# Transformer block and graph attention in fp32: the handover from attention to feed-forward reordered

## The reference

```python
# condition c: [B, 128]; mod gives shift, scale and gate for both halves
x = x + g_msa * attention(modulate(layernorm(x), sh_msa, sc_msa), W_qkv, W_out, b_out)
x = x + g_mlp * (gelu(modulate(layernorm(x), sh_mlp, sc_mlp) @ W1 + b1) @ W2 + b2)
# then a graph attention over the first 20 nodes with the integer mask adj [B, T, T, 11]:
#   twice: softmax(q k / sqrt(8) where adj.sum(-1) > 0, + adj @ w_bias) applied to the features, @ Wout
x = x + relu(self_feat + graph_attention_0 + graph_attention_1)
```

## Time and profile before

| | |
|---|---|
| median of 3 runs | 643.64 us (642.64 to 646.8) |
| profiled execution | 646.53 us, its span 645.0 us |
| TensorE busy | 626.7 us, 97% of the span |
| VectorE / ScalarE / GpSimd busy | 507.7 / 480.8 / 290.1 us |
| granted clock of TensorE over the span | 0.99 |
| handover looked at here | about 404 to 431 us |

### The profile page before, as it was taken

How to read it: one execution, slowest core, us unless ns; L and a number is a source line. 1 busy time by engine, 2 the same in 40 slices (tenths; PEclk the granted TensorE clock), 3 DMA queues, 4 the chain that set the end, 5 groups by cost and what they waited for, 6 DMA issues and landing times.

```text
span 645.0 us, 17285 instructions
## 1 busy us (share of the span) xinstructions
PE 626.7 (97%) x5560; PEld 542.2 (84%) x5560; DVE 507.7 (79%) x1116; ACT 480.8 (75%) x1722; POOL 290.1 (45%) x354
## 2 busy tenths in 40 slices
PE   8999999999999999999999999889998999999996
PEld 7778888888888888888888888779897888888875
DVE  4887887878788778878787886977866888888874
ACT  4888877877978878788779788768776565656552
POOL 3353444443452534544434524546554444554451
PEclk9999999999999999999999999999999999999996
DMA  7212011010110110110111102013341122112100
GB/s 240 61 29 54 10 46 44 18 44 22 38 44 8 44 52 8 44 44 17 44 28 33 44 1 63 25 59 111 101 135 59 45 67 67 43 55 65 49 27 24
DMA packets 54530, 32.50 MB, mean 50 GB/s; under 512 B 15184, under 2 KB 52320, under 8 KB 54496
## 3 DMA queue, kind: packets, MB, share of 16 engines
q1 hardware_dynamic: 52864, 27.85, 15.7%
q0 software_dynamic: 1632, 4.21, 2.0%
HBM read 25.74 MB, written 6.31 MB: 50 GB/s over the span
## 4 chain that ended last, share of the span: by engine, by line
PE 88%; DVE 6%; SPq 2%; ACT 2%; issue 1%; DMA 0%; ACTq 0%; DVEq 0%
PE banks L601 10%; PE banks L627 9%; PE banks L612 8%; PE banks L1890 7%; PE banks L572 6%; PE banks L576 4%; PE banks L573 4%; PE banks L1306 4%; PE banks L1862 3%; PE banks L585 3%; PE banks L1876 3%; PE banks L1850 2%; PE banks L648 2%; PE banks L649 2%; PE banks L587 2%; PE banks L650 2%
## 5 line engine op out<-in xcount | busy, mean ns | idle before, releaser
L518 POOL TENSOR_TENSOR late_blocks<-late_blocks,p_rsum 128x512 f32<-128x512 f32 x128 | 130.5, 1040 | 209.3 <-DVE p_rsum L934 209.3
L813 ACT ACTIVATE late_blocks<-banks,neg_max 128x128 f32<-128x128 f32 x512 | 182.8, 392 | 2.4 <-DVE neg_max L927 2.4
L813 ACT ACTIVATION_READ_ACCUMULATOR late_blocks<-banks,neg_max 128x1 f32 x512 | 119.1, 233 | 0.0
L791 ACT ACTIVATE wide<-banks 128x512 f32<-128x512 f32 x127 | 78.4, 618 | 38.8 <-PE banks L576 34.1
L947 DVE CAST oT_hi<-banks 128x512 fp32r<-128x512 f32 x60 | 41.5, 691 | 63.9 <-PE banks L627 63.9
L572 PE MATMUL banks<-xT_hi,w_qkv_hi 128*128 128x256 f32 x256 | 82.3, 322 | 0.6 <-DVE xT_lo L922 0.6
L927 DVE TENSOR_REDUCE neg_max<-banks 128x8 f32<-128x1024 f32 x64 | 77.1, 1205 | 1.2
L601 PE MATMUL banks<-wide 64*128 64x128 f32 x1024 | 74.4, 285 | 0.0
L576 PE MATMUL banks<-xT_hi,w_qkv_lo 128*128 128x256 f32 x256 | 71.5, 279 | 0.1
L573 PE MATMUL banks<-xT_lo,w_qkv_hi 128*128 128x256 f32 x256 | 71.3, 278 | 0.0
L601 PEld LDWEIGHTS banks<-wide 64*128 64x128 f32 x1024 | 62.1, 187 | 10.7 <-issue 7.9
(11 more groups left out here) (170 smaller groups left out, 1558.5 us busy)
## 6 DMA issues: line engine op xcount, KB each, us to landing
early<-in_mask SPq DMA_DIRECT2D x16, 220.0 KB
early<-in_mask SPq DMA_DIRECT2D x80, 44.0 KB
x_in<-in_x SPq DMA_DIRECT2D x16, 128.0 KB, 2.1
x_res<-in_x SPq DMA_DIRECT2D x16, 128.0 KB, 2.2
x_scratch<-x SPq DMA_DIRECT2D x16, 128.0 KB, 1.9
f_x_in<-x_scratch SPq DMA_DIRECT2D x16, 128.0 KB, 2.4
f_x_res<-x_scratch POOLq DMA_DIRECT2D x16, 128.0 KB, 2.8
x_scratch<-f_x POOLq DMA_DIRECT2D x16, 128.0 KB, 2.2
```

The costliest lines, as they stand in the source:

```text
L518: pool.tensor_tensor(p[:, par, heads, :], p[:, par, heads, :], p_rsum[:, par, heads].unsqueeze(2).broadcast_to([128, 4, T]), ALU.mult).the ...
L791: act.activation(dst, proj_ps[k % 2], ACT.Copy).then_inc(proj_saved[k % 2], 1)
L813: act.activation(p[:, par, m, :], s_ps[par][:, e, j, :], ACT.Exp, bias=neg_max[:, par, 4 * e + j:4 * e + j + 1], accum_out=p_sum[:, par, m ...
```

## The change

- Attention's last body, TensorE: `last_probs_v(1)` comes before `turn_back(LAST)`.
- The high parts of units 0 and 1 are made by ScalarE (`save_last_oT(0)`, `(1)`) behind `cast` and in front of the load of gelu's table; VectorE makes only the low parts, both in front of the residual. ScalarE's modulation of pair 0 now stands in front of the high parts of units 2 and 3.
- The second group of unit 3 is normalised by VectorE (`normalise_last`) instead of GpSimd.
- The row maximum of unit 2 comes before the moments of pair 0. The moments of pair 1 move behind the copies of units 2 and 3. The moments of pair 2 move from the feed-forward's body 0 to behind `gate(PAIRS)`, and `sum_cells` behind these. GpSimd makes both inverse deviations (pairs 1 and 2) before `weigh`.
- TensorE: `turn(pair(1))` comes before the first layer of pair 0, `turn_back(PAIRS)` behind it. ScalarE: `modulate` of pair 1 first in body 0. VectorE: `split` of pair 1 and then `residual(PAIRS)` first in body 0.
- `f_xT_hi` and `f_xT_lo` get two buffers, and `split` waits for the products of the pair before the last.
- SyncE: pair 2 is loaded without the wait for the 15 stores (it waits for three, earlier).

```diff
@@ -509,11 +510,11 @@
             pool.tensor_tensor(rstd[:], rstd[:], ln_const[:, 1], ALU.pow).then_inc(ln_rstd_made, 1)
-        def normalise(i, unit):
+        def normalise(i, unit, groups=2):
             par = unit % 2
             pool.wait_ge(rsum_ready, i * 4 + (unit + 1))
-            for grp in range(2):
+            for grp in range(groups):
                 heads = slice(4 * grp, 4 * grp + 4)
                 pool.tensor_tensor(p[:, par, heads, :], p[:, par, heads, :],
@@ -545,13 +546,13 @@
             ffn.parts["rstd_first"](pool)
             normalise(LAST, 2)
-            normalise(LAST, 3)
+            normalise(LAST, 3, groups=1)
             ffn.parts["rstd_second"](pool)
             edges.parts["weigh"](pool, LAST)
         run_bodies(pool, body, last_body)
-    def tensor(pe):
+    def tensor(pe, turn_back_only=False):
         def turn_x(i):
@@ -705,7 +706,10 @@
         def turn_last(unit, grp):
-            pe.wait_ge(p_ready, LAST * 8 + (2 * unit + grp + 1))
+            if grp == 1 and unit == 3:
+                pe.wait_ge(last_p_ready, 1)
+            else:
+                pe.wait_ge(p_ready, LAST * 8 + (2 * unit + grp + 1))
             if grp == 0 and unit == 0:
                 pe.wait_ge(turn_saved[0], LAST * 8 + 1)
@@ -749,8 +753,8 @@
             ffn.parts["turn_first"](pe)
             last_probs_v(0)
+            last_probs_v(1)
             turn_back(LAST)
-            last_probs_v(1)
             turn_last(2, 0)
             turn_last(2, 1)
@@ -758,6 +762,9 @@
             last_probs_v(3)
+        if turn_back_only:
+            turn_back(PAIRS)
+            return
         setup.tensor(pe)
         turn_x(-1)
@@ -783,7 +790,6 @@
         run_bodies(pe, body, last_body)
         project_out(PAIRS)
-        turn_back(PAIRS)
     def scalar(act):
@@ -856,6 +862,12 @@
                 save_v(i, V1[0], 1, 0)
+        def save_last_oT(unit):
+            half, b = unit // 2, unit % 2
+            act.wait_ge(turn_full[0], LAST * 8 + WEIGHTED[unit])
+            act.activation(oT_hi[:, 4 * half:4 * half + 4, b, :],
+                           last_ps[unit % 2].rearrange("p (c t) -> p c t", c=4), ACT.Copy).then_inc(oT_high, 1)
+
         def last_body():
@@ -864,18 +876,16 @@
             exps(LAST, 3, 0, 8)
             edges.parts["cast"](act, LAST)
+            save_last_oT(0)
+            save_last_oT(1)
             ffn.parts["load_gelu"](act)
             save_turned(LAST, 2)
...
             act.activation(last_pT[1][:, 4:8, :].rearrange("p m t -> p (m t)"), t_ps[1],
                            ACT.Copy).then_inc(turn_saved[1], 1)
-            for unit in (2, 3):
-                half, b = unit // 2, unit % 2
-                act.wait_ge(turn_full[0], LAST * 8 + WEIGHTED[unit])
-                act.activation(oT_hi[:, 4 * half:4 * half + 4, b, :],
-                               last_ps[unit % 2].rearrange("p (c t) -> p c t", c=4),
-                               ACT.Copy).then_inc(oT_high, 1)
             ffn.parts["modulate_first"](act)
+            save_last_oT(2)
+            save_last_oT(3)
         setup.scalar(act)
...
@@ -1031,18 +1041,23 @@
             src = last_ps[unit % 2].rearrange("p (c t) -> p c t", c=4)
             hi = oT_hi[:, 4 * half:4 * half + 4, b, :]
-            if unit < 2:
-                dve.wait_ge(turn_full[0], LAST * 8 + WEIGHTED[unit])
-                dve.tensor_copy(hi, src).then_inc(oT_high, 1)
             dve.wait_ge(oT_high, LAST * 4 + (unit + 1))
             dve.tensor_tensor(oT_lo[:, 4 * half:4 * half + 4, b, :], src, hi.bitcast(F32),
                               ALU.subtract).then_inc(turn_saved[0], 1)
+        def normalise_last():
+
+            dve.wait_ge(rsum_ready, LAST * 4 + 4)
+            heads = slice(4, 8)
+            dve.tensor_tensor(p[:, 1, heads, :], p[:, 1, heads, :],
+                              p_rsum[:, 1, heads].unsqueeze(2).broadcast_to([128, 4, T]),
+                              ALU.mult).then_inc(last_p_ready, 1)
+
         def last_body():
             invert_sums(LAST, 1)
+            row_max(LAST, 2)
             ffn.parts["moments_first"](dve)
-            row_max(LAST, 2)
             save_last(0, 0)
             save_last(0, 1)
@@ -1051,19 +1066,24 @@
             ffn.parts["normalise_first"](dve)
             invert_sums(LAST, 3)
+            normalise_last()
             gate(LAST)
             save_last_oT(0)
+            save_last_oT(1)
             residual(LAST)
-            save_last_oT(1)
             save_last(2, 0)
             save_last(3, 0)
-            edges.parts["sum_cells"](dve, LAST)
+            ffn.parts["moments_second"](dve)
             save_last_oT(2)
             save_last_oT(3)
             ffn.parts["split_first"](dve)
             gate(PAIRS)
+            ffn.parts["moments_third"](dve)
+            edges.parts["sum_cells"](dve, LAST)
+
+        if residual_only:
             residual(PAIRS)
-
+            return
         for n in range(2):
...
@@ -1152,8 +1173,8 @@
     gate_cols = sb("f_gate_cols", [128, 2, 2, COLS])
     xT = sb("f_xT", [128, 2, T])
-    xT_hi = sb("f_xT_hi", [128, 2 * T], F32R)
-    xT_lo = sb("f_xT_lo", [128, 2 * T], F32R)
+    xT_hi = sb("f_xT_hi", [128, 2, 2 * T], F32R)
+    xT_lo = sb("f_xT_lo", [128, 2, 2 * T], F32R)
     hT = g.wide[:, 0:2 * MCH * 2 * T].rearrange("p (n c t) -> p n c t", n=2, c=MCH)
@@ -1215,12 +1236,12 @@
         if first:
-            sp.wait_ge(g.x1_stored, 2 * 16)
+            sp.wait_ge(g.x1_stored, 3 * 16)
             load_x(Step(0, 0))
             load_x(Step(0, 1))
             return
+        body(Step(-1, 0))
         sp.wait_ge(g.x1_stored, (PAIRS - 1) * 16)
-        body(Step(-1, 0))
         store_last_x1(sp)
         run_bodies(sp, body, start=-1)
@@ -1241,7 +1262,7 @@
         def body(s):
-            if more(s, 2) and not at(s, -1):
+            if more(s, 2) and not at(s, 0):
                 rstd_of(step_from(s, 2))
             if more(s, -2):
@@ -1253,6 +1274,7 @@
         if part == "second":
             rstd_of(Step(0, 1))
+            rstd_of(Step(1, 0))
             return
         if part == "first":
@@ -1292,9 +1314,9 @@
             for c in range(first, first + 2):
                 dst, cols = hid_ps[s.par][:, c, :], slice(c * 128, c * 128 + 128)
-                pe.matmul(dst, g.w1_hi[:, cols], xT_hi[:], start=True, stop=False)
-                pe.matmul(dst, g.w1_hi[:, cols], xT_lo[:], start=False, stop=False)
-                last = pe.matmul(dst, g.w1_lo[:, cols], xT_hi[:], start=False, stop=True)
+                pe.matmul(dst, g.w1_hi[:, cols], xT_hi[:, s.par], start=True, stop=False)
+                pe.matmul(dst, g.w1_hi[:, cols], xT_lo[:, s.par], start=False, stop=False)
+                last = pe.matmul(dst, g.w1_lo[:, cols], xT_hi[:, s.par], start=False, stop=True)
             last.then_inc(hid_full, 1)
@@ -1318,10 +1340,12 @@
             if more(s, 0):
                 hidden(s, 0)
-            if more(s, 1):
+            if more(s, 1) and not at(s, 0):
                 turn(step_from(s, 1))
             if more(s, 0):
                 hidden(s, 2)
+            if at(s, 0):
+                turn_back_last(pe)
             if more(s, -2):
                 turn_back(step_from(s, -2))
@@ -1331,6 +1355,7 @@
             return
+        turn(pair(1))
         run_bodies(pe, body, stop=PAIRS - 1)
@@ -1399,9 +1424,11 @@
         def body(s):
+            if at(s, 0):
+                modulate(step_from(s, 1))
             if more(s, 0):
                 gelu(s, 0)
-            if more(s, 1):
+            if more(s, 1) and not at(s, 0):
                 modulate(step_from(s, 1))
             if more(s, 0):
@@ -1462,10 +1489,11 @@
             dve.wait_ge(modulated, s.n + 1)
-            zero_wait(dve, hid_full, s.n * 2)
-            dve.tensor_copy(xT_hi[:], flat).then_inc(xT_split, 1)
+            zero_wait(dve, hid_full, s.n * 2 - 2)
+            dve.tensor_copy(xT_hi[:, s.par], flat).then_inc(xT_split, 1)
             dve.wait_ge(xT_split, s.n * 2 + 1)
-            dve.tensor_tensor(xT_lo[:], flat, xT_hi[:].bitcast(F32), ALU.subtract).then_inc(xT_split, 1)
+            dve.tensor_tensor(xT_lo[:, s.par], flat, xT_hi[:, s.par].bitcast(F32),
+                              ALU.subtract).then_inc(xT_split, 1)
         def residual(s):
@@ -1488,7 +1516,10 @@
         def body(s):
-            if more(s, 2) and not at(s, -1):
+            if at(s, 0):
+                split(step_from(s, 1))
+                residual_last(dve)
+            if more(s, 2) and not at(s, 0):
                 moments(step_from(s, 2))
             if more(s, 1) and not at(s, 0):
@@ -1515,12 +1546,17 @@
             normalise(Step(0, 0))
             copy_cols(mod_cols, Step(0, 0), mod_cols_ready)
+            return
+        if part == "second":
             moments(Step(0, 1))
             return
...
             normalise(Step(0, 1))
             copy_cols(mod_cols, Step(0, 1), mod_cols_ready)
+            return
```

(2 more changed lines are left out.)

22 lines of the change are left out of this document (13 added, 9 removed).

## The result

The changed kernel takes **650.25 us** (median of 15 runs, 647.49 to 651.98); the kernel before, in runs on the same chip beside it, takes 645.08 us (15 runs, 642.64 to 648.33). The ratio is 1.0077 with an interval of 1.0061 to 1.0092: about 5.0 us slower, where 2.6 was forecast, and beyond the upper end of the range. The forecast of 646.2 stood on a median of three runs, 643.64; the median of 15 is 1.44 higher.

A forecast was written before the change was run, and what follows sets the result against it. TensorE, busy 97% of the span, was taken to bound, with the third pair's first products deciding. Part 1 gave 0; the held low part and late load gave +2.6 on 643.64: 646.2 us, range 643.0 to 648.0.

The forecast's parts named there:

- The base: Median time of the kernel before, 643.64 us, to which the forecast shift of 2.6 us was added.
- What bounds: Attention to feed-forward handover: when the third pair's first products start on TensorE decides; at most 4.11 us to gain.
- Part 1, gain 0: Both weighings at once, high parts on ScalarE: projection ends at 422.57 as before; 0.6 us gain without contention.
- one of the two orders that were named: VectorE beside GpSimd: normalising product held, or gate columns' copy behind it; both put the gating about 1.0 us later.
- The walk: Step-by-step times from the gating at 413.65 to the projection's end at 422.57; the 1.28 us table load costs nothing.
- Part 2, the held low part: VectorE's low part of the second pair's split, held by GpSimd's weighing, ends 427.34; products start 427.4, 0.35 us later.
- Part 3, the late load: Fourth pair's load, issued behind the last residual, puts the third pair's first products at 433.05 instead of 430.43: +2.6 us.
- landed + 2.4: Fourth pair's load lands 2.4 us, the median, after its issue at 428.2, so at 430.6.
- the 0.7 us more: Allowance for GpSimd's two residual loads sharing queues with the fourth pair's load; landings range from 2.1 to 3.1.
- rival "worse": GpSimd's loads push the landing past 3.1 us and two GpSimd products delay the gating: +4 and more; chance 0.06.
- TensorE's own work doesn't bind: Handover: products from 427.4 plus 3.40 us of TensorE's steps give 430.8, ahead of the third pair's split at 433.05.

The follow-up runs named there:

- e4_norm: Changed kernel with both groups of the last unit normalised on GpSimd again, none on VectorE; 649.75 us, ratio 1.01.
- e1_cells: Changed kernel with the sum of cells, and with it GpSimd's weighing, back ahead of the last two low parts; 645.99 us, ratio 1.0007.
- f1_warm: e10_hold_res plus one more 128 KB load that nothing reads, issued on SyncE's queue ahead of the last store; 648.72 us, ratio 1.005.
- c1_after: The changed kernel once more, unedited, for a second profile; 650.87 us, ratio 1.0075.
- e5_awake: Changed kernel with 18 unread identity products on TensorE in the pause behind the last pair's turn back; 649.56 us, ratio 1.0063.
- e3_cells_load: Changed kernel with the sum of cells and GpSimd's weighing moved back, and the fourth pair's load ahead of the last store; 642.56 us, ratio 0.9961.
- e7_all: Changed kernel with sum of cells and weighing moved back, fourth pair's load ahead of the last store, GpSimd normalising both groups; 641.52 us, ratio 0.9951.
- e8_res_early: Changed kernel with GpSimd's two residual loads issued before the third pair's inverse deviation; 648.44 us, ratio 1.0061.
- e10_hold_res: Changed kernel with GpSimd's two residual loads issued early and the fifth pair's load held until the fourth pair's moments are made; 649.07 us, ratio 1.0055.
- e9_hold_fifth: Changed kernel with the fifth pair's load held in SyncE's queue until the fourth pair's moments are made; 650.01 us, ratio 1.009.

## Why the prediction was wrong in size and right in mechanism

**The base.** 650.25 is 4.05 above the forecast of 646.2. 1.44 of it is the base, the median of three runs; the other 2.6 are the shift. Without either the base's 1.44 or the 1.63 of the landing below, the time would still lie above the range's end of 648.0, and without both inside it.

**What bounds: right.** When the third pair's first products start decided it; the distance explains 4.0 to 4.25 of the 5.0 us.

**Part 1, gain 0: right.** The gate columns' copy was held for 1.00 us behind the normalising product, one of the two orders that were named. TensorE's last projection product comes 0.64 us earlier than before (421.65 against 422.29), but at 402 us, where the two kernels still do the same, this execution is already 0.63 us ahead, so nothing was won. Without the contention it would have been 0.82 us (e4_norm), where 0.6 was forecast. The walk had the table load in front of the copy cost nothing; ScalarE's copy waits for TensorE (0.70 us) and not for the load, as said.

**Part 2, the held low part: right, to the tenth.** Forecast to end 0.29 us after the weighing, it ended 0.27 after it, and e1_cells shows the cause: 0.42 us without the weighing. The Trainium skill (SBUF — State Buffer, section "SBUF: two separate sides") calls it an exclusive lock for the whole instruction, between a VectorE instruction with two SBUF inputs and a GpSimd instruction that reads SBUF. The 2.04 agrees with that, as far as the start goes: the held subtraction ended 0.27 us behind the weighing, less than its own 0.42.

**Part 3, the late load: right in every step but one.** From the end of the last projection product (forecast 422.57, measured 421.93) the sum stands like this:

| step | forecast, us | measured, us |
|---|---|---|
| to the residual's end | 427.75 - 422.57 = 5.18 | 427.01 - 421.93 = 5.08 |
| to the load's issue | 0.46 | 0.50 |
| **landing** | **2.4** | **4.02** |
| statistics to the third pair's products | 2.45 | 434.04 - 431.53 = 2.51 |
| sum | 10.48 | 12.11 |

The whole miss of this sum, 1.63 us, is **the term "landed + 2.4"**, the median of the earlier trace rows; even the row's maximum, 3.1, which is the 0.7 us more that the prediction allowed for GpSimd's loads, was too little. The prediction put these loads on the same queues as this one; the profile has them on another (q0 against q1), and what they share is the 16 DMA engines. The two loads of this tile behind the last store of before took 2.3 and 3.1 us; the second had the 16 KB packet beside it, which the prediction didn't look for. The rival "worse" named this crowding past 3.1, with 0.06, and asked for a second delay in the gating that didn't occur.

**"TensorE's own work doesn't bind": true only because the load was later still.** The prediction's own numbers put a pause of about 3 us on TensorE, from the turn back to 427.4, and its 3.40 us of steps were taken at full clock. The clock in the earlier trace rows is 1.00 throughout, and the prediction didn't ask what a longer pause would do to it. It fell to half at 425.9, 0.28 us products took 0.41, and the steps took 6.45 us (426.74 to 434.04, less the wait of 0.85) instead of 3.40. They would have held the third pair's products to 433.19. With a landing of 2.4 us the load's chain would have been ready at 432.42, so TensorE would have bound, 0.8 us later than the sum. f1_warm is close to that case: with a landing of 3.2 us its steps take 6.40 (428.85 to 435.25) and TensorE waits for nothing in front of the third pair's products.

**From +4.2 to +5.0.** The changed kernel's profiled span is 5.0 us longer than before's; at the third pair's products it was 3.61 us later (434.04 against 430.43). At the last residual of the feed-forward it is 4.07 later (496.35 against 492.28), and at the second reciprocal of the graph phase (`g_r_sum`) 5.17 (509.20 against 504.03). Between these two its windows have a clock of 0.76 and 0.90. In c1_after, whose clock is 1.00 there, the same two points are 4.41 and 4.51 later. So a fall of the clock near 500 us is worth about 1 us in the executions that have it, which e5_awake repeats (5.69 and 6.79 later).

**The end of the kernel.** In every trace the clock falls to half in the last bodies of the graph phase and stays there, and it matters when: before's profile has it from 632.3 us on, e1_cells' from 638.9, and e1_cells goes from 1.4 us behind before at 626 us to 1.7 us ahead at the end. A median mixes such executions. In 100 runs of the kernel before beside the experiments, the 34 with a mean granted clock of 0.996 or above took 643.2 us in the median and the 51 with 0.985 to 0.991 took 646.6. The prediction's base lay near the first group and its profiled execution in the second. Of the changed kernel's 15 runs only one has a clock of 0.996, and it took 647.49: 4.2 us more at a like clock, which is the distance. So the rest of the 5.0 us goes with the clock, in the trace and in the runs; where it fell in the runs without a trace is not known.

## What to carry to other kernels

Before moving a product on VectorE or GpSimd, lay the two engines' timelines side by side: a subtraction of 0.43 us that begins 0.15 us after GpSimd's costs GpSimd's whole length, and the place of the step that releases GpSimd counts for more than the length of VectorE's queue. Follow what is behind the held instruction into SyncE's queue: a load that had 0.1 us of room needs its own place in the order, independent of the store, as in e3_cells_load and e7_all, where the same reordering is faster than before. And take a landing from loads that had the company that this one will have, not from the median of all: here the one load of 3.1 us had an instruction packet beside it, at 428.0 us, and the change put the load that counts beside the same packet, now at 427.7. Before medians a few us apart are compared, the runs' mean granted clocks should be.

## What the runs showed of the hardware that was not expected

- **The same pause lowers the clock in some executions only.** Ten traced executions have a pause of 2.99 to 3.00 us in front of the second pair's products. In eight TensorE's clock fell to the half level (1.2 GHz), in the pause or within 2 us behind it: in the changed kernel 0.59 of full from 425 to 430 us. In e8_res_early and e10_hold_res it didn't, though a second pause of 3.13 and 3.10 us follows there. e8_res_early:

```profile
425.00:430.00 5.00, 3.45 (x22) 3.09 (x22) 2.34 (x4) 0.84 (x2) 1.21 (x1) 1.00 0.29 79
430.00:435.00 5.00, 1.87 (x15) 1.60 (x14) 3.24 (x14) 2.83 (x8) 0.88 (x2) 1.00 0.01 4
```

  And e5_awake, with the first pause filled, fell at the end of the later wait of 2.53 us instead (0.73 from 435 to 440). In this one execution the fall came with the next pause.
- **Both sides of the VectorE and GpSimd hold pay**: GpSimd's product, 1.03 us alone, took 1.54 when VectorE's began 0.04 us ahead of it, and VectorE's next copy of 4 columns then took 1.00 instead of 0.12.
- **A 128 KB load of the same tile took from 2.1 us (the least in the earlier trace rows) to 4.1 us (e9_hold_fifth) to land**, and an edit of the transfers around it brought at most 0.6 us of that back. Most of what is left goes with one 16 KB packet of the instruction queue, by the traces: in e10_hold_res the 34 packets of one DMA engine's share start only when it ends, 1.2 us behind the other 510.
- **The last bodies run at half clock, and from when decides up to 3 us**: 632.3 us in before's profile, 638.9 in e1_cells'.
